# An RWKV recurrence rewritten as a weighted mean, inside a fused adaLN + RWKV + MoE block

## The chip, the core and the metric

The kernel runs on one core of a Trainium2 chip. Its engines run side by side and are ordered only by semaphores: PE (TensorE, matrix products), DVE (VectorE) and ACT (ScalarE) for elementwise work, POOL (GpSimd), and SP, which here only issues transfers. Each engine takes its own instructions strictly in the order in which the program lists them. The metric is the device time of one execution in microseconds (us); lower is better.

## What is computed

x is 4 sequences of 1024 tokens with 256 channels, float32. Six modulation vectors come from `silu(c) @ wmod`. The rest, cut to what matters:

```python
h = layernorm(x) * (1 + ca) + sa
xk, xv, xr = (x_prev + (h - x_prev) * t for t in (tmk, tmv, tmr))   # x_prev is h one token earlier
k, v, r = xk @ Wk.T + bk, xv @ Wv.T + bv, xr @ Wr.T + br
# over the tokens, for each channel, decay = -exp(time_decay), bonus = time_first:
ww = bonus + kt;  p = maximum(pp, ww);  e1 = exp(pp - p);  e2 = exp(ww - p)
out = (e1 * aa + e2 * vt) / (e1 * bb + e2)
ww2 = pp + decay; p2 = maximum(ww2, kt); e1 = exp(ww2 - p2); e2 = exp(kt - p2)
aa, bb, pp = e1 * aa + e2 * vt, e1 * bb + e2, p2
x = x + ga * ((sigmoid(r) * out) @ Wo.T + bo)
h = layernorm(x) * (1 + cb) + sb
x = x + gb * (moe(h) + silu(h @ sWg) * (h @ sWu) @ sWd)   # 8 experts of width 64, top 2, and a shared one
```

## The kernel before

Tokens are cut into 8 chunks c0 to c7 of 512 tokens, two for each sequence; the second of a pair starts from the state that the first left. On the recurrence side the channels lie on the partitions (two halves of 128, called h or kc) and the tokens along the free axis, so that one DVE scan instruction runs 512 steps of a recurrence.

For each chunk the stages are: `stats1` (DVE) and rstd (POOL), `normalise1` (ACT), `turn1` (PE transposes), `affine1` (ACT), `part_mix` (ACT) and `mix` (DVE), `project` (PE: six products, K in two halves, then V, then R; two products of 128x512 for each), `add_bias` and `tanh_r` (ACT), the recurrence (DVE and ACT), `attn` (PE), `residual1`, `stats2`, `normalise2`, `turn2`, `affine2`, `low_part` (DVE, line 1241: the low part of h2, which the feed-forward products need), then `logits`, `route`, ten products `up` (i = 0 to 9, six matmuls each), `silu`, `gate_up`, `spread_comb`, `weigh`, `down` and `residual2`.

The recurrence of one chunk before: on DVE `scan_max` (running maximum, and the difference `tmp` to it), `scan_sums` (bb, aa), `out_sums` (den and num in five operations of 128x1024) and `divide` (four more: one Newton step on the reciprocal, and the factor 1 + tanh(r/2), whose result is `rw`, line 1219).
The order of all work is written out by hand in one list for each engine: an unrolled start, a loop over chunks, an unrolled end. A list interleaves the recurrence of chunk n+1 with the feed-forward part of chunk n-1 or n. Instructions wait on counting semaphores, so an instruction that is not ready holds all that is listed behind it on its engine. PSUM has eight banks: mm0 to mm3 for project and up, yo0 and yo1 for attn and down, tp and cb for transposes, logits and combining weights. Loads of x wait on SP for `residual1` of three chunks earlier, and in some places stand behind the loading of the gate rows, which waits for `down_weight` and `out_weight`.

## Time and profile before

| | us |
|---|---|
| median of 3 runs | 391.45 |
| the runs | 391.04, 391.45, 394.34 |
| time of the profiled execution | 391.8 |
| its span | 390.0 |
| mean granted clock of TensorE | 0.964 of full |

| engine | busy us | share | instructions |
|---|---|---|---|
| PE | 355.2 | 91% | 1461 |
| DVE | 336.6 | 86% | 627 |
| ACT | 286.7 | 74% | 446 |
| POOL | 41.8 | 11% | 74 |

The span is cut into 40 slices on the page; a digit is the busy share in tenths. The first seven slices (about 68 us) are the fill, in which chunk 0 passes through the stages alone; the last four are the drain.

```
PE   3994592799999999999999999999999999989986
DVE  5689999989999999999999899998999999851541
ACT  2579998878986899879885998699795987133210
PEclk9879796699999999999999999999999999999999
```

Matmul records overlap, since they are pipelined, so the sum of their mean durations says less than the distance from one start to the next. A float32 product appears as two records.

### The profile page before, as it was taken

To read this page: it belongs to the slowest core of one execution; us is meant where nothing else is said; L and a number is where in the kernel's file an instruction comes from. 1 tells how busy PE (TensorE), PEld (TensorE's weight loads), DVE (VectorE), ACT (ScalarE), POOL (GpSimd) and SP (SyncE) were. 2 spreads that over 40 slices of the span, in tenths; PEclk is the share of its full clock that TensorE was granted. 3 is DMA by queue.
4 is the path that set the end of the run, shared out by engine and by line. 5 is a ranking of instruction groups with operands and counts; after the bars stand their busy time and mean duration, and the time that the engine had idled before them with its cause. 6 is when DMAs were issued, how large, how long until landed. Compare 5 with 4: busy or idle time off the path is not lost.

```text
span 390.0 us, 4478 instructions
## 1 busy us (share of the span) xinstructions
PE 355.2 (91%) x1461; PEld 254.6 (65%) x1461; DVE 336.6 (86%) x627; ACT 286.7 (74%) x446; POOL 41.8 (11%) x74
## 2 busy tenths in 40 slices
PE   3994592799999999999999999999999999989986
PEld 3942251468687758767766757776866767868765
DVE  5689999989999999999899999998999999851541
ACT  2579998878986899879885998699795987133210
POOL 3200006000400022002300040002300200010000
PEclk9879796699999999999999999999999999999999
DMA  8940020000003000102003000103010000100011
GB/s 274 257 146 3 0 68 26 0 2 1 0 2 108 0 1 2 54 2 72 22 2 109 0 2 0 54 3 94 0 50 6 0 1 2 54 0 2 0 54 55
DMA packets 16239, 14.87 MB, mean 38 GB/s; under 512 B 4766, under 2 KB 15192, under 8 KB 16216
## 3 DMA queue, kind: packets, MB, share of 16 engines
q1 hardware_dynamic: 16184, 14.58, 11.9%
q8 instruction: 12, 0.20, 0.2%
q14 instruction: 11, 0.09, 0.1%
q10 hardware_dynamic: 32, 0.01, 0.0%
HBM read 10.38 MB, written 4.21 MB: 37 GB/s over the span
## 4 chain that ended last, share of the span: by engine, by line
PE 47%; DVE 28%; ACT 12%; issue 7%; DMA 4%; POOL 1%; SPq 0%; DVEq 0%; ACTq 0%; POOLq 0%
PE mm L869 16%; PE yo L900 11%; PE mm L771 7%; PE yo L797 4%; DMA x_in<-in_L_attn_x_dram 3%; DVE state L1154 3%; DVE mixed L1136 3%; ACT arg L429 3%; DVE n_stats L1121 2%; PE tp L721 2%; ACT n_xn L364 2%; PE yo L909 2%; DVE act L1309 1%; DVE state L1173 1%; DVE state L1176 1%
## 5 line engine op out<-in xcount | busy, mean ns | idle before, releaser
L771 PE MATMUL mm<-mixed,WT 128*128 128x512 f32 x192 | 92.1, 624 | 5.7 <-DVE mixed L1136 5.7
L900 PE MATMUL yo<-WdG,act 128*128 128x256 f32 x320 | 70.8, 379 | 1.4 <-DVE act L1309 1.4
L771 PEld LDWEIGHTS mm<-mixed,WT 128*128 128x128 f32 x192 | 37.7, 202 | 45.6 <-issue 37.0
L900 PEld LDWEIGHTS yo<-WdG,act 128*128 128x128 f32 x320 | 60.2, 190 | 10.3 <-DVE act L1309 1.9
L869 PE MATMUL mm<-h_h,w_up_h 128*128 128x512 f32 x160 | 52.2, 407 | 0.0
L869 PE MATMUL mm<-h_h,w_up_l 128*128 128x512 f32 x160 | 50.4, 396 | 0.0
L869 PE MATMUL mm<-h_l,w_up_h 128*128 128x512 f32 x160 | 50.3, 395 | 0.0
L474 ACT ACTIVATE pool_g<-mm 128x512 f32<-128x512 f32 x40 | 23.6, 590 | 27.6 <-PE mm L869 27.5
L336 POOL TENSOR_TENSOR n_ve<-n_mv,small 128x4 f32<-128x4 f32 x16 | 5.3, 334 | 298.3 <-DVE n_mv L1125 298.3
L1136 DVE SCALAR_TENSOR_TENSOR mixed<-hT,cols,mixed 128x512 f32<-128x512 f32 x48 | 33.8, 746 | 1.3 <-ACT mixed L423 1.3
L869 PEld LDWEIGHTS mm<-h_l,w_up_h 128*128 128x128 f32 x160 | 30.0, 188 | 7.3
L869 PEld LDWEIGHTS mm<-h_h,w_up_l 128*128 128x128 f32 x160 | 30.0, 188 | 7.3
L869 PEld LDWEIGHTS mm<-h_h,w_up_h 128*128 128x128 f32 x160 | 28.7, 188 | 7.1 <-DVE pool_g L1302 0.6
L423 ACT ACTIVATE mixed<-hT,rest 128x512 f32<-128x512 f32 x48 | 31.4, 715 | 0.0
L797 PE MATMUL yo<-WoG,pool_n 128*128 128x256 f32 x128 | 28.9, 379 | 0.0
L721 PE MATMUL tp<-ident,n_xn 128*128 128x128 f32 x88 | 14.9, 296 | 13.6 <-ACT n_xn L364 10.9
L412 ACT ACTIVATE kv<-mm,cols 128x512 f32<-128x512 f32 x32 | 21.6, 678 | 7.1 <-PE mm L771 6.8
L721 PEld LDWEIGHTS tp<-ident,n_xn 128*128 128x128 f32 x88 | 11.3, 152 | 23.5 <-ACT n_xn L364 14.9
L797 PEld LDWEIGHTS yo<-WoG,pool_n 128*128 128x128 f32 x128 | 24.3, 190 | 3.6
L1302 DVE TENSOR_TENSOR pool_g<-mm,pool_g 128x512 f32<-128x512 f32 x32 | 21.9, 684 | 4.1 <-PE mm L869 2.6
L339 POOL TENSOR_TENSOR n_rstd<-n_ve,small 128x4 f32<-128x4 f32 x16 | 21.8, 1363 | 1.3
L1154 DVE TENSOR_TENSOR_SCAN state<-decay,state,kv 128x512 f32<-128x512 f32 x16 | 20.5, 1281 | 0.7 <-ACT kv L412 0.3
(160 smaller groups left out, 627.3 us busy)
## 6 DMA issues: line engine op xcount, KB each, us to landing
x_in<-in_L_attn_x_dram SPq DMA_DIRECT2D x8, 512.0 KB, 5.0
out_dram<-pool_x SPq DMA_DIRECT2D x5, 512.0 KB, 2.9
gate_rows<-gate_dram SPq DMA_DIRECT2D x4, 384.0 KB, 4.2
...
```

Source lines behind the costliest of these rows:

```text
L339: nc.gpsimd.tensor_tensor(norm.rstd[:, :], norm.ve[:, :], small[:, 1, :], ALU.pow).then_inc(norm.rstd_done if direct else norm.pool_step, 1)
L412: nc.scalar.activation(kv[:, w, kc, :], mm[PROJECT_BANK[j]][:, :], ACT.Identity, bias=bias_cols[w][:, kc:kc + 1]).then_inc(kv_done, 1)
L423: nc.scalar.activation(mixed[:, w, kc, :], hT[c.half][:, kc, 0:CH], ACT.Identity, scale=rest[:, KH * w + kc:KH * w + kc + 1]).then_inc(par ...
L474: nc.scalar.activation(sg[:, e, :], mm[UP_BANK[2 * e]][:, :], ACT.Silu).then_inc(silu_done, 1)
L721: last = nc.tensor.transpose(dst[:, t * P:(t + 1) * P], norm.xn[:, t, kc * P:(kc + 1) * P], ident[:, :])
L771: last = nc.tensor.matmul(mm[PROJECT_BANK[j]][:, :], WT[:, w, kc, oc * P:(oc + 1) * P], mixed[:, w, kc, :], start=(kc == 0), stop=(kc == K ...
L797: last = nc.tensor.matmul(yo[k][:, (t % 2) * H:(t % 2 + 1) * H], rw[:, kc, t * P:(t + 1) * P], WoG[:, kc, :], start=False, stop=(kc == KH ...
L869: last = nc.tensor.matmul(mm[UP_BANK[i]][:, :], w[:, kc, gu, e * P:(e + 1) * P], rhs[:, kc, :], start=(n == 0), stop=(n == 3 * KH - 1))
L900: last = nc.tensor.matmul(dst, act[:, e, t * P:(t + 1) * P], WdG[:, e, :], start=(e == 0), stop=(e == NB - 1))
L1136: nc.vector.scalar_tensor_tensor(out=mixed[:, w, kc, :], in0=hT[c.half][:, kc, 1:CH + 1], scalar=mix_cols[w][:, kc:kc + 1], in1=mixed[:, w ...
L1154: nc.vector.tensor_tensor_scan(state[:, 0, h, 1:CH + 1], decay[:, h:h + 1].to_broadcast([P, CH]), kv[:, K, h, :], state[:, 0, h, 0:1], ALU ...
L1302: nc.vector.tensor_tensor(dst[:, e, :], mm[UP_BANK[2 * e + 1]][:, :], sg[:, e, :], ALU.mult).then_inc(prod_done, 1)
```

## The change

The state (aa, bb, pp) becomes (pp, bb', mean): pp as before, bb' a sum of exponentials that starts at 1 so that its logarithm exists, and the mean aa/bb itself. The share with which a new value enters the mean is a logistic function of (k - pp) - ln(bb') plus a constant, computed as 1 + tanh of half of it; the output is the previous mean plus such a share of (v - mean). So there is no denominator, no seed, no Newton step.

* DVE: `out_sums` and `divide` go. In come `offset` (tmp minus the logarithm, 128x512 for each half), `share_value`, `scan_weight` and `scan_mean` in place of `scan_sums`, `out_mean` (three operations of 128x1024) and `receive` (128x1024, gives `rw`).
* ACT: `output_falls`, `output_exponential` and `reciprocal_seed` go. In come `log_weight`, `tanh_state`, `keep_share` and `tanh_out`, each 128x512 for each half.
* `rw` has a tile of its own. `WT[O]` is scaled by 0.25 where it was -0.5. New waits guard the tiles that are used again (`mean_done`, `keep_done`, `value_done`, `moved_done`, `diff_done`, `out_tanh`, `state_tanh`).
* The lists of PE, ACT and DVE are written anew over the whole kernel; more chunks are unrolled at the start.

The new functions (the old bodies stand above):

```diff
                 w, kc = divmod(j, KH)
                 ac.wait_ge(kvr_mm, 3 * KH * c.n + j + 1)
+                if w == V:
+                    wait(ac, diff_done, c.n)
...
+            @of_chunk
+            def state_falls(c, h):
+                wait(ac, mean_done, KH * (c.n - 1) + h + 1)
                 ac.wait_ge(gain_done, KH * c.n + h + 1)
-                nc.scalar.activation(arg[:, j, h, :], tmp[:, h, :], ACT.Relu, scale=sign, bias=bias[:, h:h + 1]
-                                     ).then_inc(relu_done, 1)
...
-            def output_falls(c):
-                for j, sign, bias in ((2, 1.0, col["tf"]), (3, -1.0, minus_tf)):
-                    for h in range(KH):
-                        fall_of(c, j, h, sign, bias)
...
-            def output_exponential(c, j):
-                ac.wait_ge(relu_done, 4 * KH * c.n + KH * (j + 1))
-                nc.scalar.activation(arg[:, j, :, :], arg[:, j, :, :], ACT.Exp, scale=-1.0).then_inc(exp_done, 1)
...
-            def reciprocal_seed(c):
-                ac.wait_ge(den_done, c.n + 1)
-                nc.scalar.activation(rec, den, ACT.Ln).then_inc(ln_done, 1)
-                ac.wait_ge(ln_done, c.n + 1)
-                nc.scalar.activation(rec, rec, ACT.Exp, scale=-1.0).then_inc(rec_done, 1)
+            def log_weight(c, h):
+                wait(ac, keep_done, KH * (c.n - 1) + h + 1)
+                wait(ac, value_done, KH * (c.n - 1) + h + 1)
+                ac.wait_ge(weight_done, KH * c.n + h + 1)
+                nc.scalar.activation(arg[:, 2, h, :], state[:, 2, h, 0:CH], ACT.Ln).then_inc(log_done, 1)
+            @of_chunk
+            def tanh_state(c, h):
+                ac.wait_ge(offset_done, KH * c.n + h + 1)
+                nc.scalar.activation(arg[:, 2, h, :], tmp[:, h, :], ACT.Tanh, scale=0.5, bias=half_fall[:, h:h + 1]
+                                     ).then_inc(state_tanh, 1)
+            @of_chunk
+            def tanh_out(c, h):
+                wait(ac, moved_done, c.n)
+                ac.wait_ge(offset_done, KH * c.n + h + 1)
+                nc.scalar.activation(arg[:, 3, h, :], tmp[:, h, :], ACT.Tanh, scale=0.5, bias=half_tf[:, h:h + 1]
+                                     ).then_inc(out_tanh, 1)
+            @of_chunk
+            def keep_share(c, h):
+                if c.n == 0 and h == 0:
+                    ac.wait_ge(consts_done, 6)
+                ac.wait_ge(state_tanh, KH * c.n + h + 1)
+                nc.scalar.activation(arg[:, 0, h, :], arg[:, 2, h, :], ACT.Identity, scale=-0.5, bias=small[:, 3, 0:1]
+                                     ).then_inc(keep_done, 1)
             @of_chunk
...
+            def seed(c, j, first, done):
+                if c.half:
+                    nc.vector.tensor_copy(state[:, j, :, 0:1], state[:, j, :, CH:CH + 1]).then_inc(done, 1)
+                else:
+                    nc.vector.memset(state[:, j, :, 0:1], first).then_inc(done, 1)
+                ve.wait_ge(done, c.n + 1)
...
-                    else:
-                        nc.vector.memset(state[:, 0, :, 0:1], START)
-                        nc.vector.memset(state[:, 1:3, :, 0:1], 0.0).then_inc(seed_done, 1)
-                    ve.wait_ge(seed_done, c.n + 1)
+                    wait(ve, gain_done, KH * c.n)
+                    seed(c, 0, START, max_seeded)
...
+            def scan_weight(c, h):
+                if h == 0:
+                    wait(ve, log_done, KH * c.n)
+                    seed(c, 2, 1.0, weight_seeded)
+                ve.wait_ge(exp_done, 2 * KH * c.n + 2 * h + 2)
+                nc.vector.tensor_tensor_scan(state[:, 2, h, 1:CH + 1], arg[:, 0, h, :], arg[:, 1, h, :],
+                                             state[:, 2, h, 0:1], ALU.mult, ALU.add).then_inc(weight_done, 1)
+            @of_chunk
+            def offset(c, h):
+                ve.wait_ge(gain_done, KH * c.n + h + 1)
+                ve.wait_ge(log_done, KH * c.n + h + 1)
+                nc.vector.tensor_tensor(tmp[:, h, :], tmp[:, h, :], arg[:, 2, h, :], ALU.subtract
+                                        ).then_inc(offset_done, 1)
+            @of_chunk
+            def share_value(c, h):
                 ve.wait_ge(kv_done, 4 * c.n + KH + h + 1)
...
+                ve.wait_ge(state_tanh, KH * c.n + h + 1)
+                nc.vector.scalar_tensor_tensor(out=arg[:, 1, h, :], in0=arg[:, 2, h, :], scalar=1.0,
+                                               in1=kv[:, V, h, :], op0=ALU.add, op1=ALU.mult
+                                               ).then_inc(value_done, 1)
+            @of_chunk
+            def scan_mean(c, h):
+                if h == 0:
+                    wait(ve, wkv_done, c.n)
+                    seed(c, 1, 0.0, mean_seeded)
+                ve.wait_ge(keep_done, KH * c.n + h + 1)
+                ve.wait_ge(value_done, KH * c.n + h + 1)
+                nc.vector.tensor_tensor_scan(state[:, 1, h, 1:CH + 1], arg[:, 0, h, :], arg[:, 1, h, :],
+                                             state[:, 1, h, 0:1], ALU.mult, ALU.add).then_inc(mean_done, 1)
+            @of_chunk
+            def out_mean(c, n):
                 if n == 0:
...
+                    wait(ve, wkv_done, c.n)
+                    ve.wait_ge(mean_done, KH * (c.n + 1))
+                    ve.wait_ge(kv_done, 4 * (c.n + 1))
+                    nc.vector.scalar_tensor_tensor(out=ev[:, :, :], in0=mean_prev, scalar=-0.5, in1=v_all,
+                                                   op0=ALU.mult, op1=ALU.add).then_inc(diff_done, 1)
                 elif n == 1:
...
+                    ve.wait_ge(diff_done, c.n + 1)
+                    ve.wait_ge(out_tanh, KH * (c.n + 1))
+                    nc.vector.scalar_tensor_tensor(out=ev[:, :, :], in0=arg[:, 3, :, :], scalar=1.0, in1=ev[:, :, :],
+                                                   op0=ALU.add, op1=ALU.mult).then_inc(moved_done, 1)
+                else:
+                    ve.wait_ge(moved_done, c.n + 1)
                     wait(ve, attn_mm, KH * c.n)
...
+                    nc.vector.tensor_tensor(rw[:, :, :], ev[:, :, :], mean_prev, ALU.add).then_inc(wkv_done, 1)
+            @of_chunk
+            def receive(c):
+                ve.wait_ge(wkv_done, c.n + 1)
+                ve.wait_ge(sgm_done, KH * (c.n + 1))
+                nc.vector.scalar_tensor_tensor(out=rw[:, :, :], in0=sgm[:, :, :], scalar=1.0, in1=rw[:, :, :],
+                                               op0=ALU.add, op1=ALU.mult).then_inc(rw_done, 1)
             @of_chunk
```

Three places of the lists. First PE from its second instruction on: `modulation` (yo from condT), `turn_square` (a weight transposed out of `act`), `turn_columns` (rows), `turn1` of chunks 0 and 1 (n_xn), and the first `project` (mixed, WT). Before:

```order
L909 MATMUL yo<-condT,pool_x 128x4 x8
L933 MATMUL mm<-ident,act 128x128 x4
L927 MATMUL mm<-ident,rows 128x18
L933 MATMUL yo<-ident,act 128x128 x4
L933 MATMUL mm<-ident,act 128x128 x4
L721 MATMUL tp<-ident,n_xn 128x128 x4
L721 MATMUL cb<-ident,n_xn 128x128 x4
L909 MATMUL yo<-condT,pool_x 128x4 x16
L771 MATMUL mm<-mixed,WT 128x512 x2
L947 MATMUL yo<-ident,gate_cols 24x128
```

And of the change:

```order
L1021 MATMUL yo<-condT,pool_x 128x4 x8
L833 MATMUL tp<-ident,n_xn 128x128 x4
L833 MATMUL cb<-ident,n_xn 128x128 x4
L1039 MATMUL mm<-ident,rows 128x18
L1045 MATMUL mm<-ident,act 128x128 x8
L1045 MATMUL yo<-ident,act 128x128 x4
L1045 MATMUL mm<-ident,act 128x128 x4
L1053 MATMUL cb<-ident,gw 128x8 x2
L883 MATMUL mm<-mixed,WT 128x512 x4
L1021 MATMUL yo<-condT,pool_x 128x4 x16
L833 MATMUL tp<-ident,n_xn 128x128 x4
L833 MATMUL cb<-ident,n_xn 128x128 x4
```

The transposes of chunk 0 moved ahead of the weights', and both K projections of chunk 0 ahead of the second modulation group.

Second DVE from the operation that writes rw of chunk 0 to the statistics of norm 2 of chunk 0 (n_stats from pool_x); `mixed` is `mix` of chunk 1. Before:

```order
L1219 SCALAR_TENSOR_TENSOR pool_n<-sgm,pool_n 128x1024
L1148 COPY state<-state 128x6
L1154 SCALAR_TENSOR_TENSOR state<-decay,state,kv 128x512
L1159 TENSOR_TENSOR tmp<-kv,state 128x512
L1136 SCALAR_TENSOR_TENSOR mixed<-hT,cols,mixed 128x512 x2
L1154 SCALAR_TENSOR_TENSOR state<-decay,state,kv 128x512
L1159 TENSOR_TENSOR tmp<-kv,state 128x512
L1227 TENSOR_TENSOR pool_x<-yo,x_in 128x512 x2
L1136 SCALAR_TENSOR_TENSOR mixed<-hT,cols,mixed 128x512 x2
L1121 BN_STATS n_stats<-pool_x 128x6 x4
```

And of the change:

```order
L1407 SCALAR_TENSOR_TENSOR rw<-sgm,rw 128x1024
L1315 COPY state<-state 128x2
L1332 SCALAR_TENSOR_TENSOR state<-decay,state,kv 128x512
L1337 TENSOR_TENSOR tmp<-kv,state 128x512
L1307 SCALAR_TENSOR_TENSOR mixed<-hT,cols,mixed 128x512 x2
L1415 TENSOR_TENSOR pool_x<-yo,x_in 128x512
L1332 SCALAR_TENSOR_TENSOR state<-decay,state,kv 128x512
L1337 TENSOR_TENSOR tmp<-kv,state 128x512
L1415 TENSOR_TENSOR pool_x<-yo,x_in 128x512
L1292 BN_STATS n_stats<-pool_x 128x6 x4
```

The pair of `mix` that stood before the statistics moved behind them, and each half of `residual1` (pool_x from yo) stands where its product of PE is ready.

Third PE at the seam of two loop rounds: the last three projections (of chunk 5), `turn2` of chunk 4 (tp and cb), `down` of chunk 3 (yo from WdG), `turn1` of chunk 6 (tp), logits (16x512), and `up` (mm from h_h). Before:

```order
L771 MATMUL mm<-mixed,WT 128x512 x6
L721 MATMUL tp<-ident,n_xn 128x128 x4
L721 MATMUL cb<-ident,n_xn 128x128 x4
L900 MATMUL yo<-WdG,act 128x256 x20
L721 MATMUL tp<-ident,n_xn 128x128 x4
L771 MATMUL mm<-mixed,WT 128x512 x2
L721 MATMUL tp<-ident,n_xn 128x128 x4
L808 MATMUL cb<-h_h,gw_hl 16x512
L810 MATMUL cb<-h_l,gw_hl 8x512
```

And of the change:

```order
L883 MATMUL mm<-mixed,WT 128x512 x6
L833 MATMUL tp<-ident,n_xn 128x128 x4
L1012 MATMUL yo<-WdG,act 128x256 x10
L833 MATMUL cb<-ident,n_xn 128x128 x4
L1012 MATMUL yo<-WdG,act 128x256 x10
L833 MATMUL tp<-ident,n_xn 128x128 x4
L981 MATMUL mm<-h_h,w_up_h 128x512 x2
L981 MATMUL mm<-h_l,w_up_h 128x512 x2
L981 MATMUL mm<-h_h,w_up_l 128x512 x2
L833 MATMUL tp<-ident,n_xn 128x128 x4
L920 MATMUL cb<-h_h,gw_hl 16x512
```

The sixth projection joined the others ahead of turn2, the two halves of turn2 and down alternate, and the first `up` stands between the two turn1.

## Rows read from the trace of the kernel before

**Rows 1.** The page, part 1: busy time, share of the span, instructions.

```profile
PE 355.2 (91%) x1461; PEld 254.6 (65%) x1461; DVE 336.6 (86%) x627; ACT 286.7 (74%) x446; POOL 41.8 (11%) x74
```

**Rows 2.** Windows: from:to, span, busy (count) of PE, PEld, DVE, ACT, POOL; clock; DMA.

```profile
70.00:80.00 10.00, 9.41 (x32) 6.05 (x33) 7.98 (x10) 8.60 (x14) 0.00 (x0) 0.73 0.00 0
...
130.00:172.40 42.40, 41.97 (x177) 30.36 (x176) 40.87 (x76) 37.13 (x59) 4.89 (x8) 1.00 0.04 13
...
257.20:299.70 42.50, 42.02 (x177) 30.25 (x176) 40.19 (x73) 35.37 (x55) 5.27 (x8) 1.00 0.11 35
```

**Rows 3.** Lines, all engines: shapes, count, busy us and mean ns, idle before.

```profile
L443 ACT ACTIVATE arg<-arg 128x512 f32<-128x512 f32 x32 | 18.4, 622 | 0.1
...
L455 ACT ACTIVATE arg<-arg 128x1024 f32<-128x1024 f32 x16 | 16.2, 1047 | 0.0
...
L1170 DVE TENSOR_TENSOR ev<-arg,kv 128x512 f32<-128x512 f32 x16 | 10.7, 668 | 0.0
...
L1214 DVE SCALAR_TENSOR_TENSOR pool_n<-tmp,ev 128x1024 f32<-128x1024 f32 x8 | 9.8, 1222 | 0.1
```

**Rows 4.** Timeline of PE, the fill: start us, us, instruction, idle before.

```profile
18.59 3.78 PE L771 MATMUL mm<-mixed,WT 128*128 128x512 f32 x4
...
41.69 5.17 PE L771 MATMUL mm<-mixed,WT 128*128 128x512 f32 x8 [5.43 <-DVE mixed L1136]
...
63.63 1.11 PE L721 MATMUL tp<-ident,n_xn 128*128 128x128 f32 x4 [5.08 <-ACT n_xn L364]
...
70.59 1.12 PE L721 MATMUL tp<-ident,n_xn 128*128 128x128 f32 x4 [4.99 <-ACT n_xn L364]
...
76.37 0.71 PE L869 MATMUL mm<-h_h,w_up_h 128*128 128x512 f32 x2
```

**Rows 5.** Windows of PE, 2 us each: busy (count), granted clock, DMA.

```profile
38.00:40.00 2.00, 0.00 (x0) 0.50 0.01 4
...
44.00:46.00 2.00, 2.00 (x5) 0.83 0.00 0
...
74.00:76.00 2.00, 2.00 (x4) 0.65 0.00 0
```

**Rows 6.** Timeline of DVE, the fill.

```profile
47.39 1.23 DVE L1219 SCALAR_TENSOR_TENSOR pool_n<-sgm,pool_n 128x1024 f32<-128x1024 f32 x1
...
50.66 1.41 DVE L1136 SCALAR_TENSOR_TENSOR mixed<-hT,cols,mixed 128x512 f32<-128x512 f32 x2
...
56.43 1.40 DVE L1121 BATCH_NORM_STATS2 n_stats<-pool_x 128x6 f32<-128x256 f32 x4
...
67.66 1.22 DVE L1241 TENSOR_TENSOR h_l<-pool_x,h_h 128x1024 fp32r<-128x1024 f32 x1 [0.69 <-ACT pool_x L404]
```

**Rows 7.** Timeline of ACT, the fill.

```profile
52.13 1.28 ACT L565 ACT_TABLE_LOAD   x1
53.43 1.15 ACT L443 ACTIVATE arg<-arg 128x512 f32<-128x512 f32 x2
...
61.50 2.07 ACT L364 ACTIVATE n_xn<-pool_x,n_shift,n_rstd 128x256 f32<-128x256 f32 x4 [0.92 <-POOL n_shift L347]
...
64.84 0.78 ACT L403 ACTIVATE h_h<-tp,modc 128x512 fp32r<-128x512 f32 x1 [0.32 <-PE tp L721]
```

**Rows 8.** Timeline of PE, a stall of the loop.

```profile
285.62 0.66 PE L721 MATMUL tp<-ident,n_xn 128*128 128x128 f32 x4 [0.48 <-ACT hT L388]
```

**Rows 9.** Timeline of all engines, the drain.

```profile
349.76 0.63 PE L721 MATMUL tp<-ident,n_xn 128*128 128x128 f32 x4 [1.68 <-DVE act L1309]
...
376.23 0.69 DVE L1302 TENSOR_TENSOR pool_g<-mm,pool_g 128x512 f32<-128x512 f32 x1 [0.79 <-PE mm L869]
...
377.78 8.90 PE L900 MATMUL yo<-WdG,act 128*128 128x256 f32 x40 [1.42 <-DVE act L1309]
```

**Rows 10.** The chain, in order of time: one plain stretch of PE.

```profile
309.07 1.41 PE mm L869 x6
```

More of the change, by code:

```diff
@@ L1000, in _ @@
             spread_comb(c0, 4)
[L1001 removed]
+            project(c2, (3, 4))
             turn2(c1, 0)
             turn2(c1, 1)
+            project(c2, (5,))
             down(c0, 0)
             down(c0, 1)
[L1008 removed]
+            turn1(c3, 0)
+            up(c1, 0)
+            up(c1, 1)
+            turn1(c3, 1)
+            up(c1, 2)
+            logits(c1)
+            up(c1, 3)
+            up(c1, 4)
+            up(c1, 5)
+            turn_logits(c1)
@@ L1533, in _ @@
             gate_up(c1, 2)
+            route(c1, 8, ROUTE_STEPS + 1)
             stats2(c2)
+            scan_max(c3, 1)
             weigh(c1, 1)
-            for n in range(2, 5):
-                prev, cur, nxt, after = (chunk(n + d) for d in (-1, 0, 1, 2))
-                down_weight(prev)
+            mix(c3, 2)
+            gate_up(c1, 3)
+            weigh(c1, 2)
+            stats1(c4)
+            gate_up(c1, 4)
+            weigh(c1, 3)
+            weigh(c1, 4)
+            scan_weight(c3, 0)
@@ new lines, in _ @@
+            offset(c4, 0)
+            weigh(c2, 4)
+            stats1(c5)
+            offset(c4, 1)
+            share_value(c4, 0)
+            scan_mean(c4, 0)
+            share_value(c4, 1)
+            scan_mean(c4, 1)
+            residual2(c2, 0)
+            low_part(c3)
+            out_mean(c4, 0)
+            out_mean(c4, 1)
+            residual2(c2, 1)
+            out_mean(c4, 2)
+            mix(c5, 0)
+            route(c3, 0, 4)
+            gate_up(c3, 0)
+            route(c3, 4, 8)
```

868 lines of the change are left out of this document (510 added, 358 removed).

## The prediction

> **What bounds the kernel now.** I read the page's busy shares first. PE has 91%, DVE 86%, ACT 74% [rows 1], which leaves PE and DVE as candidates. The shares are averages over a fill, a steady part and a drain, so the windows come next. In the steady part (130 to 299.7 us, four chunks of 42.4 us) PE is busy 41.97 to 42.02 us of each 42.4 to 42.5 at full clock, DVE 40.2 to 40.9, ACT 35.4 to 37.1 [rows 2], of which the first and the last of the four windows stand there. Matmul records overlap, so the busy sum could flatter PE; the spacing shows that it doesn't: six records of one `up` take 1.41 us [rows 10], 0.235 each, with nothing between them and the next. PE is the bound there and a lighter DVE can win back only the 0.4 us of idle in each chunk. The chain through the same stretch names many DVE and ACT lines, since a nearly full PE and a nearly full DVE can be walked either way; I go by the windows.
>
> Eight chunks of 42.0 us are 336 us of PE work at full clock. The execution takes 391.8. The other 56 us are what can be won: the fill, the drain, stalls, and stretches at half clock. In the fill the first projection starts at 18.59 [rows 4]. After it PE idles 5.4 us before 41.69, 5.1 before 63.63, 5.0 before 70.59 [rows 4]. From 70.59 on it does not idle. These gaps cost twice: the granted clock is 0.50 at 38 to 40 and 0.83 at 44 to 46, 0.73 over 70 to 80, and still 0.65 in 74 to 76 [rows 2, 5], so 1.2 GHz for some 4 us after each restart. One projection, four records, takes 3.78 us at half clock [rows 4], so 1.9 at full.
>
> **What the change takes from DVE and ACT.** DVE loses nine operations of 128x1024 for each chunk and two of 128x512 (the products ev) and gains four of 128x1024 and four of 128x512; six scans stay six. A 128x1024 one lasts 1.22 us, a 128x512 one 0.67 [rows 3], and back to back each overlaps the next by 0.08. So 5 x 1.14 - 2 x 0.59 = 4.5 us less DVE in each chunk, 36 in all. All operations but one form are in the trace: a scalar_tensor_tensor of two streams is there with 1.22 for 1024 columns [rows 3], as long as the plain products. ACT loses four relu of 128x512 and four operations of 128x1024 (1.05 us), and gains eight of 128x512 (0.6) [rows 3]: 6.2 - 4.7 = 1.5 less. Table loads stay four in each chunk of the loop. Of the 36 us on DVE nearly all lies beside PE's work in the steady part and is worth nothing there.
>
> **The fill**, placed by hand from both lists with these durations. (a) The columns (biases, decay) are ready on DVE about 2.2 us earlier, since two weight copies and the copy of V's weight moved behind them. The first projection then starts at 16.3 for 18.59. (b) K0 ends at 19.7 (half clock), K1 at 21.5, the second modulation group follows until 25.5. scan_max of both halves ends at 24.0. On ACT normalise1(c1), four relu and four exp end at 28.6; scan_weight ends at 30.0, the offsets at 31.3; ln, a table load of 1.28 [rows 7] and tanh end at 33.1, keep_share at 34.9, scan_mean at 36.9, out_mean with one mix pair (1.33) between at 41.6 behind tanh_out (38.7), out_weight and rw at 43.7. Before, rw is ready at 47.39 + 1.23 = 48.6 [rows 6]: 4.9 earlier. (c) From rw to the end of the norm 2 statistics the list holds two scan_max with difference (3.6), a mix pair, two residuals (1.2), statistics (1.75): 7.9, so 51.6. Before it held one mix pair more (the one at 50.66 and another behind the residuals) and the statistics ended at 58.2 (the 56.43 of [rows 6] plus the aggregates). (d) From there POOL's rstd and normalise2 take until turn2, 63.63 - 58.2 = 5.4 before [rows 4]: turn2(c0,0) at 57.0. (e) PE has idled about 6 us by then, so it is at half clock. Its list puts project(c1,3) between the halves of turn2: 0.9 + 3.8 + 0.5, second half at 62.2, affine2 (four of 0.66 in [rows 7]'s pitch, the last two behind it) at 63.6, low_part ends at 64.8. Before: 67.66 + 1.22 = 68.9 [rows 6], so 4.1 earlier. (f) PE does project(c1,4) and (c1,5) meanwhile, until 66.0, the clock back at full after some 5 us of work as in [rows 5]. Then it has `up` 0 to 5 of chunk 0, logits, and both turn1 of c2: 6 x 1.41 + 0.9 + 0.9 = 10.2, and one wait of about 0.7 (`up` 5 needs gate_up(c0,1), which stands behind receive(c1) and by my placing ends at 75.5): done at 76.9. Before, the same point is 76.37 + 6 x 1.41 = 84.8 [rows 4, 10]. **Lead: 7.9 us.**
>
> The least that I can make of it is 4.1, if all that follows low_part keeps its old distance. The most is 10.5, if the half clock is not met in (e) (1.9) and the wait in (f) is gone (0.7).
>
> **The steady part.** The stalls before add to 169.7 - 167.9 = 1.8 us over four chunks, four waits of a turn1 for ACT like the one of 0.48 [rows 8]. One `up` now stands between the two turn1, 1.4 us of cover. Walking one loop round of the new lists (PE time 0 at turn1): mix(nxt,0) is ready at 7.8 for 10.6, receive at 10.4 for 14.0, mix(nxt,2) at 27.2 for 28.2, gate_up 3 at 25.9 for 26.5, weigh 4 at 31.0 for 31.7. Everything is covered, but three margins are only 0.6 to 1.0. I take 1.2 of the 1.8 as won; bounds +1.8 and, should one thin margin bind by 0.5 in each of six chunks, -3.
>
> **The drain.** weigh(c7,3) moved behind gate_up(c7,4), and spread_comb 3 behind the last `up`. Before, from the last gate_up (376.23) to `down` (377.78) there are two operations, 1.55 us [rows 9]; now three, 0.6 more. The wait of 1.7 at 349.76 [rows 9] has the same cause in both lists and stays.
>
> **Sum**: 391.8 - 7.9 - 1.2 + 0.6 = 383.3 for an execution like the profiled one. That one is 0.35 above the median of the runs shown, so **383.0**. Bounds of the terms, from the median of 391.45: 391.45 - 10.5 - 1.8 + 0.6 = 379.8, and 391.45 - 4.1 + 3 + 0.6 = 391.0.
>
> **A rule against the ACT chain.** The table load lasts 1.28 us and the first exp starts 0.02 after it ends, at 53.43 [rows 7]; so I price a switch at 1.3. The Trainium skill (ScalarE: Activation LUTs, What ACT_TABLE_LOAD costs) puts 1.38 us of drain on top of such a load for every switch. By it the two switches that chunk 0 and 1 now have ahead of affine2(c0), ln to tanh, would each cost that more and the lead would shrink by up to 2.8 us, to a time of 385.8. The row shows no such gap, so the sum goes without it.
>
> **The rivals.**
> 1. DVE is the real bound: then all of the 36 us come out, 391.5 - 36 = 355.5. For it: DVE at 40.9 of 42.4 us in the steady part. Against it: PE has no idle time to give back, and 336 of its work behind a first projection at 16.3 fill 352 before the drain's waits and the last store. 3%.
> The Trainium skill (Perfetto Trace Analysis, Identifying the Most-Contended Engine) says that matmul busy time is no fair measure and to use the weight loads' share; by that, 65% against DVE's 86% [rows 1], this rival would be the forecast. The spacing of 0.235 us in [rows 10] speaks against it here.
> 2. The fill gives little: PE's idle merges into a longer one ahead of turn2(c0,0), the half clock lasts through projections and first `up`, and the thin margins bind. Then only low_part's 4.1 comes through, less 2 to 4: 388 to 393. 13%.
> 3. Slower: the new recurrence crosses between ACT and DVE six times for each chunk (relu, scan, ln, offset, tanh, scan, output) where the old one crossed three times, on engines that run in list order. In my round tanh_out ends at 41.3 and out_mean behind it at 44.2, route starts at 46.7 and receive has 3.6 us of margin to attn. If the chain runs more than those 3.6 us late, PE waits in each round; with 3 us of wait in six rounds, +18 - 9: 400. It decides against the change from 1.5 us of wait in each round on. 6%.
> 4. The lead is fuller than I place it and no stall stays: 378 to 380. 10%.
> 5. The forecast, 380 to 387.5: 68%.
>
> **How the numbers follow.** Leaving out 1, 3, the low part of 4 and the top of 2, the range is 379.0 to 389.0. A measurement here can tell about 1% (3.9 us) from no change. Faster by more (under 387.5): 1, 4, 5 and a trace of 2, 0.82. Within: the rest of 2 and its neighbourhood, 0.12. Slower: 0.06.
>
> **What would show it.** First projection near 16.3; turn2(c0) near 57; `up`(c0,0) near 66 to 68, and no PE idle over 1 us from there to the drain; DVE busy near 36.4 us in a steady round of 42.0; PE busy over the span unchanged in kind but its records' sum near 350. It is wrong if a round of PE takes over 42.5 us, if turn2(c0) is later than 60, or if DVE's new forms last clearly longer than 0.67 and 1.22.

## The result, and the profile after

The changed kernel takes **399.98 us** (median of 4 runs, 397.65 to 402.79) against 392.89 for the kernel before in the same session (391.04 to 395.86): ratio 1.020, 95% interval [1.015, 1.025]. The forecast of 383.0 was wrong in sign and by 17 us. The profiled execution took 400.45 us with a span of 398.6.

The page, part 1 (busy us, share of the span, instructions) and the clock in 40 slices:

```profile
PE 356.4 (89%) x1461; PEld 254.9 (64%) x1461; DVE 306.8 (77%) x616; ACT 269.9 (68%) x442; POOL 43.2 (11%) x75
...
PEclk9998968999999999899999999999996999999999
```

DVE lost 29.8 us of busy time and ACT 16.8 against [rows 1], and PE is still the busiest. Outside the fill the clock row has an 8 and a 6 where the kernel before had only 9. The windows over the stretch of [rows 2] (us, then busy and count of PE, PEld, DVE, ACT, POOL, clock, DMA):

```profile
130.00:172.40 42.40, 40.60 (x162) 28.12 (x161) 34.60 (x69) 32.47 (x55) 5.17 (x8) 0.96 0.12 35
...
257.20:299.70 42.50, 39.59 (x167) 28.39 (x166) 34.57 (x67) 34.82 (x55) 5.77 (x8) 0.99 0.04 13
```

PE, which had 42.0 busy in each 42.4, now has 39.6 to 40.6, at a clock a little under full. So the steady part itself got longer, while both engines that the change unloads have more idle time than before.

What PE waits for (engine, what it would do, who releases it: us in all, times, longest):

```profile
PE mm L981 <- DVE pool_g L1490: 11.8, 7, 3.0
PE tp L833 <- ACT n_xn L364: 8.3, 1, 8.3
```

The first row didn't exist before. L981 is `up`, L1490 is `gate_up`. PE's timeline in the last loop round (start, us, instruction, idle before and releaser):

```profile
296.16 0.63 PE L981 MATMUL mm<-h_h,w_up_l 128*128 128x512 f32 x2
299.76 1.22 PE L981 MATMUL mm<-h_h,w_up_h 128*128 128x512 f32 x2 [2.97 <-DVE pool_g L1490]
...
302.49 5.29 PE L883 MATMUL mm<-mixed,WT 128*128 128x512 f32 x8
```

The instruction at 299.76 begins `up` 5. It writes into the bank (mm3) that `up` 3's result occupies until `gate_up` 1 has read it, and `gate_up` 1 is late. DVE in the same time:

```profile
292.44 0.22 DVE L1446 TENSOR_REDUCE rt<-tp 128x32 f32<-128x64 f32 x1 [1.57 <-PE tp L932]
...
293.95 1.41 DVE L1307 SCALAR_TENSOR_TENSOR mixed<-hT,cols,mixed 128x512 f32<-128x512 f32 x2
295.27 0.68 DVE L1490 TENSOR_TENSOR act<-mm,pool_g 128x512 f32<-128x512 f32 x1
...
296.71 0.68 DVE L1509 TENSOR_TENSOR WoG<-WT,gate_rows 128x512 f32<-128x512 f32 x1
297.43 0.42 DVE L1512 TENSOR_TENSOR bias_hl<-gate_rows,bias_hl 64x256 fp32r<-64x256 f32 x1
297.88 1.23 DVE L1407 SCALAR_TENSOR_TENSOR rw<-sgm,rw 128x1024 f32<-128x1024 f32 x1
299.02 0.68 DVE L1490 TENSOR_TENSOR pool_g<-mm,pool_g 128x512 f32<-128x512 f32 x1
```

The row starts when PE's `turn_logits` (291.98, L932) releases `route` at 292.44, and from there DVE is hardly idle: `mix`, `gate_up` 0 at 295.27, then `route` 4 to 8, `out_weight`, `receive` (297.88), and only then `gate_up` 1 at 299.02. PE has run out of work at about 296.8 and starts `up` 5 at 299.76, 7.78 us behind its own `turn_logits`, with 4.8 us of work in between. In the kernel before, `gate_up` 1 stood late in DVE's list too, but `up` 5 stood behind the K projections, `attn` and `turn_comb` in PE's list, 7.7 us of cover (252.44 to 260.14 in its trace; `gate_up` 1 ended at 258.5). The change moved `up` 5 ahead of them.

The six waits of this kind after the fill are 0.92, 1.79, 1.71, 2.06, 2.97 and 0.48 us (at 121, 165, 211, 255, 300, 344), 9.9 together, and there is one of 0.75 for ACT's `silu` at 183. Two of the six cost a second time. Granted clock of PE in windows of 2 us:

```profile
166.00:168.00 2.00, 2.00 (x5) 0.50 0.00 0
168.00:170.00 2.00, 2.00 (x5) 0.66 0.00 0
...
212.00:214.00 2.00, 2.00 (x8) 1.00 0.00 0
...
256.00:258.00 2.00, 2.00 (x8) 1.00 0.00 0
...
300.00:302.00 2.00, 2.00 (x5) 0.50 0.03 8
302.00:304.00 2.00, 2.00 (x4) 0.50 0.00 0
304.00:306.00 2.00, 2.00 (x4) 0.53 0.00 0
```

Behind the waits at 165 and 300 the engine runs at 0.50, the 1.2 GHz level, and the eight records at 302.49 take 5.29 us where full clock needs 3.70. The lost share of these windows is 1.7 and 2.9 us, 4.6 together. Behind the waits at 211 and 255 nothing is lost.

**The account against the forecast**, for the profiled executions: 400.45 - 383.3 = 17.2. The lead of the fill is 4.9 instead of 7.9 (+3.0, below); waits of `up` 5 in the rounds, with the 0.75 for `silu`, +10.7; half clock +4.6; the old stalls of [rows 8] are all gone, 1.8 where 1.2 was taken (-0.6); the drain -0.2. That gives 17.5. The lead is from one execution each: the experiments below that keep the lists of the changed kernel up to `up(c0, 0)` have that instruction at 65.8 to 67.9 in their profiled executions, against 67.15 here, so it is known to about 1 us only.

### The profile page after: what moved, and what is told of

It is laid out like the page before. It is cut to its first block, busy times and chain, and to the rows that moved or that the text cites. A ratio compares the mean times of both kernels' runs of the same rounds, so it can differ in the third digit from the quotient of the medians.

```text
span 398.6 us, 4559 instructions
## 1 busy us (share of the span) xinstructions
PE 356.4 (89%) x1461; PEld 254.9 (64%) x1461; DVE 306.8 (77%) x616; ACT 269.9 (68%) x442; POOL 43.2 (11%) x75
## 3 DMA queue, kind: packets, MB, share of 16 engines
q1 hardware_dynamic: 16184, 14.58, 12.2%
## 4 chain that ended last, share of the span: by engine, by line
PE 73%; DVE 12%; ACT 7%; issue 4%; POOL 2%; DMA 1%; SPq 0%; DVEq 0%; ACTq 0%; POOLq 0%
PE mm L981 20%; PE mm L883 19%; PE yo L1012 17%; PE yo L909 6%; DVE mixed L1307 3%; PE tp L833 2%; ACT mixed L425 2%; DMA pool_x<-in_L_wmod_dram 1%; DVE pool_g L1490 1%; PE cb L993 1%; PE cb L833 1%; ACT arg L435 1%; ACT n_xn L364 1%; DVE rw L1400 1%; PE yo L1021 1%
## 5 line engine op out<-in xcount | busy, mean ns | idle before, releaser
L883 PE MATMUL mm<-mixed,WT 128*128 128x512 f32 x192 | 93.2, 628 | 7.2 <-DVE mixed L1307 7.2
L981 PE MATMUL mm<-h_h,w_up_h 128*128 128x512 f32 x160 | 54.5, 422 | 12.6 <-DVE pool_g L1490 11.8
L414 ACT ACTIVATE kv<-mm,cols 128x512 f32<-128x512 f32 x32 | 21.7, 678 | 43.7 <-PE mm L883 43.7
L981 PE MATMUL mm<-h_h,w_up_l 128*128 128x512 f32 x160 | 51.1, 401 | 0.0
L981 PE MATMUL mm<-h_l,w_up_h 128*128 128x512 f32 x160 | 50.9, 399 | 0.0
L981 PEld LDWEIGHTS mm<-h_h,w_up_h 128*128 128x128 f32 x160 | 27.9, 190 | 22.0 <-DVE pool_g L1490 14.9
L981 PEld LDWEIGHTS mm<-h_h,w_up_l 128*128 128x128 f32 x160 | 30.6, 191 | 7.4
L981 PEld LDWEIGHTS mm<-h_l,w_up_h 128*128 128x128 f32 x160 | 30.3, 190 | 7.5
L909 PE MATMUL yo<-WoG,rw 128*128 128x256 f32 x128 | 29.2, 379 | 0.0
L1497 DVE TENSOR_TENSOR act<-cb,pool_g 128x512 f32<-128x512 f32 x24 | 16.4, 682 | 14.5 <-PE cb L993 14.5
L909 PEld LDWEIGHTS yo<-WoG,rw 128*128 128x128 f32 x128 | 24.3, 190 | 4.4 <-issue 1.0
L1490 DVE TENSOR_TENSOR pool_g<-mm,pool_g 128x512 f32<-128x512 f32 x32 | 21.8, 681 | 3.8 <-PE mm L981 3.8
L1349 DVE TENSOR_TENSOR_SCAN state<-arg,state 128x512 f32<-128x512 f32 x16 | 20.3, 1282 | 4.1 <-ACT arg L443 3.9
```

The source lines that it names most:

```text
L414: nc.scalar.activation(kv[:, w, kc, :], mm[PROJECT_BANK[j]][:, :], ACT.Identity, bias=bias_cols[w][:, kc:kc + 1]).then_inc(kv_done, 1)
L883: last = nc.tensor.matmul(mm[PROJECT_BANK[j]][:, :], WT[:, w, kc, oc * P:(oc + 1) * P], mixed[:, w, kc, :], start=(kc == 0), stop=(kc == K ...
L909: last = nc.tensor.matmul(yo[k][:, (t % 2) * H:(t % 2 + 1) * H], rw[:, kc, t * P:(t + 1) * P], WoG[:, kc, :], start=False, stop=(kc == KH ...
L981: last = nc.tensor.matmul(mm[UP_BANK[i]][:, :], w[:, kc, gu, e * P:(e + 1) * P], rhs[:, kc, :], start=(n == 0), stop=(n == 3 * KH - 1))
L1349: nc.vector.tensor_tensor_scan(state[:, 2, h, 1:CH + 1], arg[:, 0, h, :], arg[:, 1, h, :], state[:, 2, h, 0:1], ALU.mult, ALU.add).then_in ...
L1490: nc.vector.tensor_tensor(dst[:, e, :], mm[UP_BANK[2 * e + 1]][:, :], sg[:, e, :], ALU.mult).then_inc(prod_done, 1)
```

## The experiments

All comparisons are with the kernel before on the same chip. Its medians there were 391.4 to 392.1.

### Move one item of DVE's list

```diff
                 gate_up(prev, 0)
+                gate_up(prev, 1)
                 route(prev, 4, 8)
                 out_weight(cur)
                 receive(cur)
-                gate_up(prev, 1)
```

The same move, to the place behind `gate_up` 0 or one item later, in six rounds (chunks 0 and 2 to 6), nothing else. It is no return to the list of before, where `gate_up` 1 stood later still.

> The changed kernel with gate_up(.,1) listed on DVE ahead of route 4 to 8, out_weight and receive (rounds of chunks 0, 2, 3, 4, 5, 6; nothing else moved). Theory A, the place in DVE's list: PE's waits for pool_g before up 5 (10.7 us after 120, 1.9 before 80) shrink to under 3 us, the half clock behind two of them (about 4.6 us) goes too, and the time falls by 11 to 17 us from 400 to 383 to 389. Rival B, the recurrence's longer chain over ACT and DVE: PE then waits for rw or mixed instead, time 396 to 401. Rival C, half clock is the cost by itself: waits go but 300 to 320 still runs at half clock, 393 to 397.

Measured: **385.87 us** (384.92 to 386.06), ratio 0.985 [0.980, 0.990]. PE's wait and one window of the loop:

```profile
PE mm L981 <- DVE pool_g L1490: 0.9, 1, 0.9
```

```profile
256.00:298.00 42.00, 42.00 (x176) 30.25 (x175) 35.85 (x72) 34.11 (x55) 5.76 (x8) 1.00 0.04 13
```

One list item takes 14 us off the changed kernel and turns slower into faster. The traces carry it: the profiled executions differ by 14.7 us, 1.2 of it already at chunk 1's `up` 5 (119.84 for 121.05); behind it 8.8 us of waits and the 4.6 of half clock are gone, 13.4 of the remaining 13.5. The round is 42.0 us of full PE, as forecast, with 35.9 to 38.2 of DVE in its four windows. There is next to no room: in the round at 288, `gate_up` 1 ends at 287.88 and `up` 5 starts at 287.96.

### A smaller dose: one place up

```diff
                 out_weight(cur)
+                gate_up(prev, 1)
                 receive(cur)
-                gate_up(prev, 1)
```

The same in the other five rounds, past the single item that stands there (`receive`, `out_weight` or `route` 4 to 8).

> A dose between the changed kernel (400 us) and e1_gate_first (385.9 us): on DVE gate_up 1 moves up by a single item in the same six rounds (in the rounds of the loop that item is receive or out_weight, or route 4 to 8, some 0.6 to 1.2 us of DVE's time). Theory (the time of the changed kernel hangs on how late gate_up 1 stands behind up 5's earliest start, one for one, and the half clock on how long PE then waits): each of the waits ahead of up 5 (0.9, 1.8, 1.7, 2.1, 3.0, 0.5 us) falls by 0.6 to 1.2 us, no wait is over 2.3 us, the half clock behind them goes or is left in one place, and the time is 389 to 393 us. Rival (the order on DVE works as a whole, by what else waits behind route and receive): the waits ahead of up 5 fall but others take their place, 395 to 400 us.

Measured: **390.13 us** (388.24 to 391.87, 10 runs), ratio 0.997 [0.994, 1.000]. The row of waits falls from 11.8 to 5.8. The longest, in the last loop round, and the clock behind it:

```profile
291.26 0.74 PE L981 MATMUL mm<-h_h,w_up_h 128*128 128x512 f32 x2 [1.85 <-DVE pool_g L1490]
```

```profile
292.00:294.00 2.00, 2.00 (x8) 1.00 0.03 8
294.00:296.00 2.00, 2.00 (x7) 1.00 0.00 0
```

2.97 became 1.85, by the 1.14 of `receive` that no longer stands ahead. 6.0 us of waits and 4.6 of half clock are gone, 10.6 in all. The profiled executions differ by 12.2, of which 1.3 arose in the fill, where the lists are the same; the medians differ by 9.9. Between no move, one place and the whole way the time is 400.0, 390.1 and 385.9: it follows the place of this one item.

### Fill the gap with work: is the half clock a cost of its own?

```diff
+                if 2 <= c.n <= 5:
+                    pe.wait_ge(x2_done, 2 * c.n)
+                    for _ in range(8):
+                        nc.tensor.matmul(yo[0][:, :], w_up_h[:, 0, 0, 0:P], h2_h[:, 0, :], start=True, stop=True)
```

This stands ahead of `up` 5 in the rounds of chunks 2 to 5. The products are extra work and never read. All lists are those of the changed kernel.

> The changed kernel with its lists as they are; in the rounds of chunks 2 to 5, PE runs 8 more 128x512 matmuls (8 x 0.235 = 1.9 us) into a bank of the output projection that is free there, just ahead of up 5, so that part of its wait for gate_up 1 is filled with work. Theory (half clock behind the wait is a cost of its own, 1.7 + 2.9 = 4.6 us in the changed kernel): the time from turn_logits to up 5 stays as it was within 0.5 us a round, since the filler takes the place of idle time, the granted clock stays at 0.9 or more behind up 5 in all rounds, and the time is 395 to 397 us against 400. Rival (the half clock has nothing to do with the gap ahead of up 5): dips remain behind it, and the time is 400 or up to 2 us more, the filler's overhang.

Measured: **396.6 us** (394.82 to 397.08, 10 runs), ratio 1.010 [1.007, 1.013]. The last loop round:

```profile
297.08 0.74 PE L985 MATMUL mm<-h_h,w_up_h 128*128 128x512 f32 x2 [1.11 <-DVE pool_g L1494]
```

```profile
298.00:300.00 2.00, 2.00 (x8) 1.00 0.00 0
300.00:302.00 2.00, 2.00 (x7) 1.00 0.00 0
```

PE does more work and the kernel is 3.4 us faster, because no window of the loop is below full clock. 2.97 of idle became 1.9 of filler and 1.11 of idle, and from the round's `turn_logits` to `up` 5 it is 7.79 us (289.29 to 297.08) where the changed kernel has 7.78 (291.98 to 299.76): the filler advances nothing. So the half clock was a separate loss; the waits are the larger part. Its size fits too: this profiled execution is 5.6 us shorter than that of the changed kernel, 1.0 of it already at chunk 1's `up` 5 (120.02 for 121.05), which leaves 4.6, as read from the windows. The windows are from one execution, the fastest of the ten. The others have no windows, but their mean granted clock, 0.974 to 0.987, is in every one above that of all four executions of the changed kernel (0.961 to 0.970).

### The other side of the wait: `up` 5 late on PE

```diff
-                up(prev, 5)
                 project(nxt, (0, 1))
                 attn(cur, 0)
                 attn(cur, 1)
+                up(prev, 5)
```

> The changed kernel with only PE's list altered: up 5 stands behind the next chunk's K projections and attn, as in the kernel before. Theory A: the 5.6 to 7 us of other work cover the gate, the waits go, 383 to 390, within 3 us of the kernel with DVE's list altered. Rival B: attn and the projections come earlier by one up and wait for rw or mixed: 394 to 401.

Measured: **402.61 us** (401.46 to 403.03), ratio 1.028 [1.023, 1.032]: a miss. PE and ACT in one round:

```profile
262.86 1.95 PE L883 MATMUL mm<-mixed,WT 128*128 128x512 f32 x4 [0.94 <-DVE pool_g L1490]
...
269.21 0.50 PE L993 MATMUL cb<-combT,sel 128*128 128x512 f32 x1 [2.54 <-ACT combT L515]
```

```profile
264.88 0.73 ACT L435 ACTIVATE arg<-tmp,decay 128x512 f32<-128x512 f32 x1 [7.55 <-DVE tmp L1337]
...
268.59 0.57 ACT L515 ACTIVATE combT<-cb 16x512 fp32r<-16x512 f32 x1
```

It is above rival B's range too, and only 1.5 us of PE's waits are for `rw`. The wait goes round a ring of three in-order lists. `up` 5 is late, so `gate_up` 2 on DVE is late, and with it V's projection (its bank, 0.94 us) and `scan_max` behind `gate_up` 2; ACT's offsets wait for `scan_max` (7.55 idle), `comb_out` stands behind them, and PE waits 2.54 for its result. The new DVE and ACT lists were made for an early `up` 5; putting it back alone breaks them. With these lists the early place is right and the place of `gate_up` 1 was not. In the kernel before, V's projections came only behind all ten `up`; a late `up` 5 with them there wasn't tried.

Both moves together:

> Both list edits. Theory A: they remove the same wait, so together no more than either alone: within 2 us of the better of the two. If there were two separate causes, the gains would add: under 380.

Measured: 403.74 us (402.29 to 405.62), ratio 1.031 [1.026, 1.037], again a miss. PE waits 7.8 us for combT in three rounds together, as above. Since `gate_up` 1 was no longer what held `up` 5, moving it bought nothing.

### The algebra in the order of before

The recurrence's new functions, put where the corresponding old ones stood; ACT's part of a round:

```diff
-                reciprocal_seed(cur)
+                tanh_state(cur, 0)
+                tanh_state(cur, 1)
+                keep_share(cur, 0)
+                keep_share(cur, 1)
+                tanh_out(cur, 0)
+                tanh_out(cur, 1)
...
-                output_falls(nxt)
...
+                log_weight(nxt, 0)
+                log_weight(nxt, 1)
```

> The new recurrence in the lists of the kernel before: PE's list word for word, on DVE the nine out_sums and divide places hold offset 0, offset 1, both share_value, scan_mean 0, scan_mean 1, out_mean 0, 1, 2 and receive, on ACT output_falls goes, the two output_exponential places hold the two log_weight, and the place of reciprocal_seed holds the table load, tanh_state, keep_share and tanh_out. Theory A (the recurrence is cheaper, the new lists lose the time): PE-bound rounds of 42 to 42.5 us as before and a fill shorter by some of DVE's 4.5 us: 385 to 391. Rival B (the new recurrence itself is slower on its longer chain): over 394.

Measured: **404.98 us** (403.5 to 407.81), ratio 1.032 [1.024, 1.039]: a miss. The costliest wait of DVE:

```profile
DVE arg L1232 <- ACT arg L460: 26.9, 7, 8.8
```

That is rival B's range, over 394. I read the wait as a matter of place: tanh stands behind two affine and two normalising groups on ACT. So the next run moved the table load, tanh and shares ahead of them:

```diff
                 log_weight(nxt, 0)
                 log_weight(nxt, 1)
+                nc.scalar.preload_act_table_set(SILU_SET)
+                tanh_state(nxt, 0)
+                tanh_state(nxt, 1)
+                keep_share(nxt, 0)
+                keep_share(nxt, 1)
                 affine2(cur, 0)
```

> The new recurrence in the lists of the kernel before, as e5_lists_before, but on ACT the tanh operations of both heads with their shares stand directly behind the logs, ahead of the two affine and normalising groups. Theory (e5 was slow since DVE's weigh waited 26.9 us for tanh results queued behind other ACT work, not since the algebra costs more): DVE's wait for tanh falls under 8 us and the time to 388 to 396 us against 404.98. Rival (the chain max, log, tanh, mix is too long wherever tanh stands): 401 to 406.

Measured: **411.23 us** (410.33 to 412.52), ratio 1.049 [1.043, 1.055]: slower still, and above both ranges. DVE's wait for tanh is 2.9 us instead of 26.9, as expected, but its wait for the second affine group (L404) went from 5.9 to 27.6, and PE waits in every round:

```profile
DVE h_l L1295 <- ACT pool_x L404: 27.6, 8, 3.7
...
DVE arg L1232 <- ACT arg L460: 2.9, 7, 1.3
```

```profile
PE tp L758 <- ACT n_xn L364: 24.8, 7, 8.4
```

Moving one group in ACT's list moved the wait instead of removing it. What these two runs show is that the algebra with two simple orders is 13 and 20 us slower than before, so it needs new lists of some kind. The changed kernel's lists, with one item moved, are one set that works. Whether some other small edit of the old lists would do is open, and so is what the new lists would give with the old algebra.

### How much slack does the chain have?

The lists of the first experiment, with one DVE operation of 128x1024 (1.22 us) that nobody needs, into a spare buffer, ahead of the last part of `out_mean` in every chunk:

```diff
+                    nc.vector.tensor_tensor(spare[:, :, :], ev[:, :, :], mean_prev, ALU.add).then_inc(spare_done, 1)
```

> The first edit (gate_up 1 ahead of receive) and one more DVE operation of 128x1024 ahead of out_mean 2 in each chunk, written to a tile that nobody reads: 1.14 us more in the chain to rw. Theory A: a round covers it (margin 3.6 us at receive by the forecast's walk), only the fill pays for it, twice: 386 + 1 to 3. Rival B, the chain bounds each round: 386 + 8.

Measured: 392.4 us (390.01 to 393.36, 10 runs), ratio 1.001 [0.997, 1.004], 6.5 above the run without it, between the two theories. In the two profiles the distance between them is 3.5 us at chunk 1's `up` 5 (123.38 against 119.84), 4.7 at 183, 5.6 at 310, and 5.5 at the end of the span. So the operations of chunks 4 to 7 cost 0.8 us together and are nearly all absorbed, while up to 183 the four of chunks 0 to 3 cost about all that they last (4.7 for 4.6 to 4.9, in a stretch that scatters by a microsecond). Theory A held for the later rounds and missed the fill and the first ones.

### What else the fill would give

Two edits on top of the first experiment: V of chunk 1 ahead of `turn2(c0)`, so that `up(c0, 0)` isn't held by it; then `residual1(c0, 1)` and `stats2(c0)` ahead of `scan_max(c1, 1)` on DVE.

```diff
-            project(c1, (2,))
+            project(c1, (2, 3))
             turn2(c0, 0)
-            project(c1, (3,))
             turn2(c0, 1)
```

> The first edit, and project(c1, 3) listed on PE ahead of both halves of turn2(c0), into the idle stretch before 59.5, instead of between them. It then runs at full clock (1.7 us for 3.4) and off the way to up(c0, 0). Theory of the fill (PE's work from turn2 to the first up bounds it): the first up comes 1.0 to 2.5 us earlier and so does the end, 383.5 to 385. Rival: low_part bounds it (it ends within 0.1 us of the last projection): under 0.5 us.

```diff
-            scan_max(c1, 1)
             mix(c1, 1)
             residual1(c0, 0)
             residual1(c0, 1)
             stats2(c0)
+            scan_max(c1, 1)
```

> As the one before, and on DVE residual1(c0, 1) and stats2(c0) ahead of scan_max(c1, 1): the statistics end 1.3 us earlier, turn2(c0, 0) by as much. If the fill's way runs over stats2 and turn2: 1 us more than the kernel without it, 382.5 to 384. Rival: the later scan_max(c1, 1) delays tanh_state(c1) and receive(c1), and attn(c1) waits for rw: nothing gained.

Measured: 385.46 us (384.34 to 386.03), ratio 0.983 [0.977, 0.989], and **384.67 us** (383.74 to 385.55), ratio 0.981 [0.975, 0.987]. The second one's fill:

```profile
59.00 1.11 PE L833 MATMUL tp<-ident,n_xn 128*128 128x128 f32 x4 [6.63 <-ACT n_xn L364]
...
66.12 0.73 PE L981 MATMUL mm<-h_h,w_up_h 128*128 128x512 f32 x2 [0.83 <-DVE h_l L1428]
```

Together the two are 1.2 us below the first experiment by the medians; each step alone is within the intervals, and both medians lie above the expected ranges. The trace doesn't settle it: `up(c0, 0)` at 66.1 lies inside the 65.8 to 67.9 that kernels without these two edits show, and with only V moved it is at 68.1.

### Small ones at the end

The drain as before on top of the first experiment (`spread_comb` ahead of `up` 8 and 9, `weigh` 3 ahead of `gate_up` 4):

```diff
-            gate_up(c7, 4)
             weigh(c7, 3)
+            gate_up(c7, 4)
```

> The lists of e1_gate_first with the order at the end of the last chunk as in the kernel before (spread_comb ahead of up 8 and 9 on PE, weigh 3 ahead of gate_up 4 on DVE). Theory, as in the prediction's term for the drain: 0.6 us less, 385.2 to 385.5 us. Rival: the end is set by the down projection alone, and the time is that of e1_gate_first, 385.9, within 0.2.

Measured: 385.31 us (384.3 to 386.91, 6 runs), ratio 0.982 [0.978, 0.987]. The median fits the 0.6 expected, but the trace doesn't carry it: from the last `gate_up` to `down` it is 1.94 us (369.73 to 371.67) in the new order and 1.89 (369.53 to 371.42) in the old. The profiled execution with the old order is 0.3 us shorter, and was 0.5 ahead at chunk 1's `up` 5 (119.37 for 119.84), so nothing of it comes from the drain. The intervals overlap as well.

All small edits together, and `gate_up` 1 ahead of `mix` 3 in the first round too:

> The lists of e8_v1_stats, with gate_up 1 ahead of mix 3 in the first loop round too (the only place where the short wait of 0.92 us ahead of up 5 was left), and the order at the end of the last chunk as in the kernel before. Theory: 0.9 us of wait and about 0.5 us at the end go, 383 to 384 us against 384.67. Rival: the delayed mix 3 of the first round moves a wait to turn_logits or the drain's chain is not on DVE's order, and the time stays at 384.5 to 386.

Measured: 384.65 us (383.25 to 385.88, 6 runs), ratio 0.980 [0.976, 0.984]. The wait of 0.92 at 118 is gone and the median is that of 384.67 without it: nothing gained that can be measured, and the rival's range. The best version found is thus 384.7 us, 2% under the kernel before.

## Why the prediction was wrong, point by point

**The step that failed is the steady part.** It says "Walking one loop round of the new lists" and then "Everything is covered, but three margins are only 0.6 to 1.0". The walk checked `mix`, `receive`, `gate_up` 3 and `weigh` 4 against their consumers, and not `gate_up` 1 against `up` 5. By the same walk `gate_up` 1 ended near 11.0 us of the round (`receive`, at 10.4, and 0.6 more), while PE stood at `up` 5 from about 9.2 on (the 10.6 at which it needs `mix(nxt, 0)`, less the 1.4 of `up` 5). The pair was 1.8 us short, and the trace has 1.7 to 3.0 in the four rounds of chunks 2 to 5. In the round of chunk 5, counted from `turn1` at 287.28, PE is at `up` 5 at 9.5 and `gate_up` 1 ends at 12.4: `receive` ends at 11.8, so the walk had also placed it 1.4 early. The wait had even been seen once, in the fill: part (f) takes 0.7 for it. In every round of the new DVE list something that `up` 5 doesn't need stands ahead of `gate_up` 1, and the step from the one wait to all of them wasn't made. The bound of -3 for thin margins also failed, since it came from the margins that were listed.

**The half clock was priced only in the fill.** The prediction notes that gaps cost twice there [rows 5] and did not apply it to a wait in the loop, having found none. It measured 4.6 us.

**The lead of the fill was 7.9; it was 4.9.** PE's timeline of the fill:

```profile
17.07 3.70 PE L883 MATMUL mm<-mixed,WT 128*128 128x512 f32 x8 [0.97 <-DVE mixed L1307]
...
45.28 0.73 PE L905 MATMUL yo<-bias_hl,bias_pick 128*128 128x512 f32 x2 [1.00 <-DVE rw L1407]
...
59.49 1.11 PE L833 MATMUL tp<-ident,n_xn 128*128 128x128 f32 x4 [8.30 <-ACT n_xn L364]
...
78.42 0.73 PE L981 MATMUL mm<-h_h,w_up_h 128*128 128x512 f32 x2 [1.91 <-DVE pool_g L1490]
```

and DVE's:

```profile
39.11 1.42 DVE L1307 SCALAR_TENSOR_TENSOR mixed<-hT,cols,mixed 128x512 f32<-128x512 f32 x2 [0.51 <-ACT mixed L425]
...
44.00 1.23 DVE L1407 SCALAR_TENSOR_TENSOR rw<-sgm,rw 128x1024 f32<-128x1024 f32 x1
...
53.38 0.28 DVE L1296 BATCH_NORM_AGGREGATE n_mv<-n_stats 128x2 f32<-128x6 f32 x3
...
65.86 1.23 DVE L1429 TENSOR_TENSOR h_l<-pool_x,h_h 128x1024 fp32r<-128x1024 f32 x1 [2.08 <-ACT pool_x L404]
```

(a) 17.07 for 16.3, made good because both K products then ran at full clock (3.70 for eight records, where [rows 4] has 3.78 for four). (b) rw at 45.2 for 43.7: the placing left out the wait for ACT's part of the `mix` at 39.11 and the small bias operation ahead of `receive`. (c) Statistics at 53.7 for 51.6, another 0.6. (d) `turn2` at 59.49 for 57.0, 0.4 more; under the 60 that was named as the limit. (e) From there to the end of `low_part` 7.6 us for 7.8, at 67.1 for 64.8, with the half clock met as assumed (0.50 in 60 to 62). (f) `up` 5 waits 1.9 instead of 0.7 and ends at 79.9 for 76.9. All links were right in kind. Most were placed a little early, and such placings add up; of the 3.0 about 1 us can be the scatter of a single execution, since with the same lists `turn2` is found at 58.6 to 60.1.

**What held.** PE is the bound: with `gate_up` 1 moved a round is 42.0 us of busy PE. The forecast for a steady round's DVE was 36.4; it is 36.9 on average there. The total of 36 us was sized too high: 29.8 came off the busy time. 1.4 us of the difference are small copies and memsets of the state that the sum left out (2.5 us for 1.1). Fewer overlapping records could give the rest; that wasn't worked out. None of it mattered, which was the claim. The new forms last as priced (name, shapes, count, busy us and mean ns, idle):

```profile
L1366 DVE SCALAR_TENSOR_TENSOR arg<-arg,kv 128x512 f32<-128x512 f32 x16 | 10.6, 680 | 3.0 <-ACT arg L460 2.6 <-ACT kv L414 0.3
...
L1395 DVE SCALAR_TENSOR_TENSOR ev<-arg,ev 128x1024 f32<-128x1024 f32 x8 | 9.8, 1222 | 1.9 <-ACT arg L469 1.8
```

The drain grew by 0.4, from 1.55 in [rows 9] to 1.95:

```profile
384.40 0.69 DVE L1490 TENSOR_TENSOR pool_g<-mm,pool_g 128x512 f32<-128x512 f32 x1 [0.19 <-PE mm L981]
```

```profile
386.35 5.88 PE L1012 MATMUL yo<-WdG,act 128*128 128x256 f32 x26 [1.58 <-DVE act L1497]
```

With only `gate_up` 1 moved, the kernel is 5.5 us under the kernel before at its side, where the sum said 8.4. The difference of 2.9 is close to the 3.0 that the lead was oversized by.

**The rule on table loads** would have taken 2.8 off the lead. ACT's timeline at such a switch:

```profile
59.97 1.28 ACT L594 ACT_TABLE_LOAD   x1
61.27 0.72 ACT L460 ACTIVATE arg<-tmp,half_fall 128x512 f32<-128x512 f32 x1
```

The operation starts 0.02 us behind the end of the load, as in [rows 7]. The Trainium skill (ScalarE: Activation LUTs, What ACT_TABLE_LOAD costs) has 1.38 us of drain there; the trace shows none, behind the load or ahead of it (the activation before ends at 59.95), so the shortfall of 3.0 isn't that.

**The rivals.** Rival 1 (DVE the bound) is out: 29.8 us less DVE, and no less time. Rival 2 had the smaller lead (4.1 us, measured 4.9) but gave 388 to 393 for the whole. Rival 3 has the right sign and, by chance, the time: it gave 400 for a chain that runs later than its margin in each round. Its form was another: `receive`, though 1.4 late in the round read above, stays inside its 3.6 us of margin to `attn`, and the wait is at a point that the rival didn't name. Its threshold, 1.5 us of wait in each round, was too high: with the one place up, some 1 us a round already takes the whole gain (390.1 against 391.4), since the lead is 3 us smaller than the sum had it. The experiments with the old lists show that the new chain, put in without care for its place, costs 13 and 20 us there; that it is the six crossings that do it is argued, not shown. 6% was too little for this rival, given one walk over lists with some forty items.
